# Layer 0's attention and its experts, two stages one after the other or one stage of turns

## The reference, cut to what matters

```python
x = x + _L0_gnn_ref(_layernorm(x), adj, W, a)            # graph attention, softmax over 64 nodes
x = x + _L0_ffn_ref(_layernorm(x), Wg, bg, W1, b1, W2, b2)
x = x + _L1_gnn_ref(_layernorm(x), adj, ...)             # three gated recurrent steps
x = x + _L1_ffn_ref(_layernorm(x), ...)                  # 16 experts of width 256, two for each token

def _L0_ffn_ref(x, Wg, bg, W1, b1, W2, b2):              # E = 8 experts, K = 2, hidden width 512
    topk_scores, topk_idx = jax.lax.top_k(x @ Wg.T + bg, K)
    combine = sum over K of softmax(topk_scores) * one_hot(topk_idx, E)
    for e in range(E):
        h = relu(x @ W1[e].T + b1[e])
        out = out + combine[..., e:e + 1] * (h @ W2[e].T + b2[e])
```

## Time and profile before

| | us |
|---|---|
| median of 3 runs | 1134.66 (1134.47 to 1137.16) |
| the profiled execution | 1134.32 |
| its span, first to last instruction | 1132.6 |
| PE busy | 977.3 (86%) |
| DVE busy | 766.8 (68%) |
| POOL busy | 601.0 (53%) |
| ACT busy | 578.4 (51%) |
| mean granted PE clock | 0.917 of 2.4 GHz |

### The profile page before, as it was taken

The page is one execution under the profiler, slowest core; times in us unless marked ns, Lnnn a source line. Parts: engine busy times, 40 slices in busy tenths (PEclk is TensorE's granted clock), DMA queues, the critical chain, the costliest instruction groups (busy, mean ns, idle before and its releaser), DMA issues. The chain is left out here.

```text
span 1132.6 us, 27053 instructions
## 1 busy us (share of the span) xinstructions
PE 977.3 (86%) x6816; PEld 802.3 (71%) x6817; DVE 766.8 (68%) x2985; ACT 578.4 (51%) x1469; POOL 601.0 (53%) x622
## 2 busy tenths in 40 slices
PE   4677776699999999859999999999985899999980
PEld 3666665499999999825555555555553789999980
DVE  3666666476666666437788888888975555555548
ACT  3777776333434343225555665565553334444455
POOL 2277777475555555510135554545545677767670
PEclk8777877699999999959999999999996899999995
DMA  9511111242222222130230321303010634333349
GB/s 229 201 49 47 49 47 54 71 115 78 70 67 72 69 69 69 41 124 0 75 89 24 96 69 54 101 29 121 25 42 31 130 107 112 93 91 90 90 143 365
DMA packets 109669, 99.08 MB, mean 87 GB/s; under 512 B 33424, under 2 KB 94480, under 8 KB 109328
## 3 DMA queue, kind: packets, MB, share of 16 engines
q1 hardware_dynamic: 92432, 62.83, 20.7%
q0 software_dynamic: 17152, 35.29, 9.3%
HBM read 55.44 MB, written 42.62 MB: 87 GB/s over the span
## 5 line engine op out<-in xcount | busy, mean ns | idle before, releaser
L1680 POOL DMA_INDIRECT result<-e_y,e_ids x280 | 280.2, 1001 | 164.2 <-issue 80.6
L415 POOL DMA_INDIRECT queue<-rows,slots x256 | 263.7, 1030 | 173.1 <-issue 121.2
L1711 PE MATMUL e_ps_h<-e_xT,e_up_of 128*128 128x128 f32 x2240 | 277.2, 278 | 3.0 <-DVE e_hT L1824 2.8
L1711 PEld LDWEIGHTS e_ps_h<-e_xT,e_up_of 128*128 128x128 f32 x2240 | 264.9, 194 | 4.0 <-issue 3.0
L1726 PE MATMUL e_ps_y<-w_sb,e_hT 128*128 x1664 | 208.3, 275 | 0.0
L1726 PEld LDWEIGHTS e_ps_y<-w_sb,e_hT 128*128 128x128 f32 x1664 | 196.8, 192 | 0.2 <-issue 0.2
L1750 ACT ACTIVATE e_hT<-e_ps_h,b_sb 128x128 f32<-128x128 f32 x272 | 77.9, 368 | 112.7 <-PE e_ps_h L1711 112.7
L1781 DVE COPY e_up_of<-w_sb 128x512 f32 x280 | 112.4, 441 | 4.1 <-issue 0.4
L1809 DVE TENSOR_SCALAR e_hT<-e_ps_h,b_sb 128x128 f32<-128x128 f32 x272 | 76.4, 343 | 32.8 <-PE e_ps_h L1711 32.6
L1824 DVE TENSOR_TENSOR e_hT<-e_ps_h,e_gate 128x512 f32<-128x512 f32 x72 | 49.7, 690 | 71.1 <-ACT e_gate L1759 71.0
L1759 ACT ACTIVATE e_gate<-e_ps_h 128x512 f32<-128x512 f32 x72 | 43.0, 597 | 96.8 <-PE e_ps_h L1711 95.5
(11 more groups left out here) (217 smaller groups left out, 1783.5 us busy)
## 6 DMA issues: line engine op xcount, KB each, us to landing
xq<-queue SPq DMA_DIRECT2D x280, 64.5 KB
g_y<-result SPq DMA_DIRECT2D x20, 512.0 KB, 4.0
result<-e_y,e_ids POOLq DMA_INDIRECT x280, 2.3
x_res<-x SPq DMA_DIRECT2D x16, 256.0 KB, 3.8
w_sb<-w SPq DMA_DIRECT2D x2, 2048.0 KB, 12.0
queue<-rows,slots POOLq DMA_INDIRECT x256, 2.5
w_sb<-w SPq DMA_DIRECT2D x16, 256.0 KB
rows<-result SPq DMA_DIRECT2D x8, 512.0 KB, 8.2
```

The costliest lines, as they stand in the source:

```text
L415: pool.indirect_dma_start(out=queue, out_offset=bass.IndirectOffsetOnAxis(ap=c.slots[q][:, k, t:t + 1], axis=0), in_=c.rows[q][:, k, t, :] ...
L1680: pool.indirect_dma_start(out=result, out_offset=bass.IndirectOffsetOnAxis(ap=ids[at_down.k][:, t, :].bitcast(U32), axis=0), in_=y[at_down ...
L1711: last = pe.matmul(ps_h[b][:, t, q * P:(q + 1) * P], up_of[at_up.k % 4][:, t, q * P:(q + 1) * P], xT[at_up.k % 4][:, t, :], start=True, st ...
```

## The change

The two stages become one, `gat_and_experts`, written out as 23 turns without a loop. In turn T, PE projects and mixes group T, turns group T-1's normalised rows, and scores and ranks T-2; four places in the turn hold an expert slot each. Slot p is in turn T, place j, with p = 4T + j - 22. In a slot's step PE turns the rows of slot p, forms the up products of p-1 and the down products of p-2 (lags of 1 and 2 in place of 2 and 4, with two buffers in place of four).

The first 56 slots are blocks of 256 rows of one expert, so that one load (1 DMA in place of 2), one copy of weights and up products with 256 columns serve both tiles; the last 12 are pairs of tiles of 128 as before, out of what is left at the end. The table is made in 14 batches of four blocks, from the counts after groups 2, 3, up to 15 (`TokenTables`, on one partition; batch b in turn b+4); the engines that need the experts' numbers load a word of each batch into a register (`TileExperts`), and SP reads the rows straight out of the table. Before the first load of a batch SP waits until the rows of group b+2 have landed.

In POOL's queue row sends and result sends take turns: two of a group, two of a slot. Attention has fewer PSUM buffers: one, `ps_t`, for all three kinds of transposes, and the projection, the scores and the ranks lie in the mix's two banks, with waits between them. Pads, the counting of landed tiles and the first loads of the next stage stay as they were, in their new places. Semaphores of the results' second half are new (`sent_first`).

```diff
+DOUBLE = 2 * P
+FOUR = 4
+DOUBLES = 56
+SINGLES = 24
+FIRST_SLOT = 22
...
-            gat_and_routing(nc, c, x, adj, gat_w, gat_wT, gat_a2, gate0_w, gate0_b, weights, small_weights, tables[0])
-            experts(nc, c, 0, c.queue0, c.result0, E0, H0 // P, up, down, up_b, down_b, tables[0], (NG - 2, NG - 1), adj, None)
+            gat_and_experts(nc, c, x, adj, gat_w, gat_wT, gat_a2, gate0_w, gate0_b, weights, small_weights, up_b, down_b)
...
+    def __call__(self, slot, t):
+        tables, tile = self.tables, slot.p if slot.double else (slot.p - DOUBLES) * PAIR + t
+        key = (slot.double, tile // FOUR)
+        if key not in self.words:
+            if slot.double:
+                self.eng.wait_ge(tables.made, tile // FOUR + 1)
+            else:
+                self.eng.wait_ge(tables.singles_made, 1)
+            source = tables.words if slot.double else tables.single_words
+            self.words[key] = self.nc.values_load_multi_w_load_instructions(
+                source[0:1, tile // FOUR:tile // FOUR + 1], engines=[self.eng.engine], min_val=0,
+                max_val=(1 << (BITS * FOUR)) - 1, skip_runtime_bounds_check_because="four experts of four bits each")[1][0]
+        return (self.words[key] >> (BITS * (tile % FOUR))) & (tables.n - 1)
...
-        ps_h = pb("ps_h", [P, GN])
-        ps_p = pb("ps_p", [P, GN])
-        ps_r = pb("ps_r", [P, GN])
-        ps_q = pb("ps_q", [P, 512])
-        scores_ps = ps_q[:, 0:G * E0]
-        ranks_ps = ps_q[:, G * E0:G * E0 + (G + 1) * E0]
+        ps_x, ps_y = (pb(name, [P, 512])[:, 0:DOUBLE] for name in ("ps_x", "ps_y"))
+        ps_up = [pb(f"ps_up{b}", [P, 512]) for b in range(2)]
+        ps_h = ps_o[:, 0, :]
+        scores_ps = ps_o[:, 0, 0:G * E0]
+        ranks_ps = ps_o[:, 1, 0:(G + 1) * E0]
...
+        def stages(T, j):
+            p = FOUR * T + j - FIRST_SLOT
+            return slot_of(p), slot_of(p - 1), slot_of(p - 2)
...
-            begin_experts(nc, sp, c, table, c.queue0, 0, E0, NG - 4)
+            for p in range(pairs):
+                slot = Slot(p)
+                if slot.double and p % FOUR == 0:
+                    batch = p // FOUR
+                    sp.wait_ge(tables.made, batch + 1)
+                    for s in range(0 if batch == 0 else batch + 2, batch + 3):
+                        wait_landed(sp, c, s % TURN, s // TURN + 1)
+                    starts = values(tables.rows, p, FOUR, E0 * REGION - DOUBLE)
+                if p == DOUBLES:
+                    sp.wait_ge(tables.padded, 16 * (E0 + 1))
+                    sp.wait_ge(tables.singles_made, 1)
+                if not slot.double and (p - DOUBLES) % FOUR == 0:
+                    starts = values(tables.single_rows, (p - DOUBLES) * PAIR, FOUR * PAIR, E0 * (REGION + P) - P)
+                if p >= HELD:
+                    sp.wait_ge(ids_copied, p - HELD + 1)
+                    alone(sp, c)
+                if slot.double:
+                    sp.dma_start(xq[p % HELD][:], c.queue0[bass.ds(starts[p % FOUR], DOUBLE), :]
...
-                    queue_rows(pool, c, c.queue0, g4.b)
-            staged(pool, body)
+            for T in range(turns):
+                for j in range(FOUR):
+                    s = group(T - 2 if j else T - 3)
+                    if s is not None:
+                        send_rows(s, 2 * (j - 1) if j else 6)
+                    at_down = stages(T, j)[2]
+                    if at_down:
+                        send_results(at_down)
...
+            def begin(slot):
+                v.wait_ge(x_turned, slot.p + 1)
+                if slot.p >= UNROLL:
+                    for t in range(PAIR):
+                        v.wait_ge(sent[t][slot.k], before[t][slot.k] + 16 * (slot.p // UNROLL))
+                v.tensor_copy(ids[slot.k][:], xq[slot.p % HELD][:, :, D:ROW]).then_inc(ids_copied, 1)
+                if slot.p >= 2:
+                    v.wait_ge(h_made, 2 * (slot.p - 1))
+                for t in range(1 if slot.double else PAIR):
+                    last = v.tensor_copy(up_of[slot.b][:, t * wide:(t + 1) * wide],
+                                         up[:, bass.ds(expert_of(slot, t) * wide, wide)])
+                last.then_inc(up_copied, 1)
...
+            def relu(slot):
+                v.wait_ge(h_made, 2 * slot.p + 2)
+                if slot.p >= 2:
+                    v.wait_ge(y_made, slot.p - 1)
+                if slot.double:
+                    for q in range(2):
+                        last = v.tensor_scalar(hT[slot.b][:, (2 + q) * DOUBLE:(3 + q) * DOUBLE],
+                                               ps_up[1][:, q * DOUBLE:(q + 1) * DOUBLE],
+                                               up_b[:, bass.ds(expert_of(slot, 0) * chunks + 2 + q, 1)], 0.0, ALU.add,
+                                               ALU.max)
...
-            staged(v, body)
+            for T in range(turns):
+                g, before_g, two_back, next_g = group(T), group(T - 1), group(T - 2), group(T + 1)
+                batch = T - 4
+                now, at_up, at_down = stages(T, 0)
+                if two_back is not None:
+                    route(two_back)
+                if now:
+                    begin(now)
+                rest(at_up, at_down)
+                if before_g is not None:
+                    update(before_g)
+                if T == NG + 2:
+                    tables.singles_1(v, c)
+                now, at_up, at_down = stages(T, 1)
+                if g is not None:
+                    attend(g)
+                if now:
+                    begin(now)
+                if two_back is not None:
+                    place(two_back)
+                rest(at_up, at_down)
+                if before_g is not None:
+                    stats(norm2, VN2, before_g)
+                    aggregate(norm2, VN2, before_g)
+                if T == NG + 2:
+                    tables.singles_2(v, c)
+                now, at_up, at_down = stages(T, 2)
+                if before_g is not None:
+                    shift(norm2, VN2, AN2, before_g)
+                if now:
+                    begin(now)
+                if next_g is not None:
+                    stats_1(next_g)
+                    aggregate(norm1, VN1, next_g)
+                rest(at_up, at_down)
+                if next_g is not None:
+                    mask(next_g)
+                if T == NG + 2:
+                    tables.singles_3(v, c)
+                if 0 <= batch < tables.batches:
+                    wait(v, VK, "carried", batch + 2)
+                    tables.doubles_1(v, c)
+                now, at_up, at_down = stages(T, 3)
+                if next_g is not None:
+                    shift(norm1, VN1, AN1, next_g)
+                if g is not None:
+                    mixed(g)
+                if now:
+                    begin(now)
+                if 0 <= batch < tables.batches:
+                    tables.doubles_2(v, c)
+                rest(at_up, at_down)
+                if 0 <= batch < tables.batches:
+                    tables.doubles_3(v, c, batch)
+                if T == NG + 2:
...
-            staged(act, body)
+            for T in range(turns):
+                g, before_g, next_g = group(T), group(T - 1), group(T + 1)
+                now, at_up, _ = stages(T, 0)
+                if g is not None:
+                    copy_turned("x", g, xnT)
+                if now:
+                    turn_out(now)
+                if at_up:
+                    relu(at_up)
+                now, at_up, _ = stages(T, 1)
+                if g is not None:
+                    copy_e(g)
+                if now:
+                    turn_out(now)
+                if g is not None:
+                    copy_h(g)
+                if at_up:
+                    relu(at_up)
+                if g is not None:
+                    exps(g)
+                if before_g is not None:
+                    inverse_std(norm2, VN2, AN2, before_g)
+                now, at_up, _ = stages(T, 2)
+                if g is not None:
+                    copy_turned("p", g, pT)
+                if now:
+                    turn_out(now)
+                if before_g is not None:
+                    normalise_2(before_g)
+                if at_up:
+                    relu(at_up)
+                if next_g is not None:
+                    inverse_std(norm1, VN1, AN1, next_g)
+                now, at_up, _ = stages(T, 3)
+                if before_g is not None:
+                    copy_turned("r", before_g, rT)
+                if now:
+                    turn_out(now)
+                if next_g is not None:
+                    normalise_1(next_g)
+                if at_up:
+                    relu(at_up)
+                if before_g is not None:
+                    copy_rows(before_g)
+                if g is not None:
+                    elus(g)
+                if T == NG + 1:
+                    act.wait_ge(product_made, 1)
```

(86 more changed lines are left out.)

690 lines of the change are left out of this document (428 added, 262 removed).

## The result

| us | before | after |
|---|---|---|
| median (lowest to highest, 4 runs each) | 1135.65 (1134.47 to 1137.16) | 1100.97 (1099.68 to 1102.61) |
| the profiled execution, its span | 1134.32, 1132.6 | 1102.61, 1100.9 |
| attention and layer 0's experts, start to PE's last down product | 10.6 to 476.8 | 10.75 to 448.0 |
| the next stage's first DVE row | 485.99 | 456.95 |
| mean granted PE clock | 0.917 | 0.929 |

The ratio is 0.9695, 95% interval 0.968 to 0.971: 34.7 us faster, where I forecast 14.3.

The account below looks back on a forecast made before the run. DVE was taken to bound the mixed turns: turn 6 begins at 110 us, ten turns of 23.3 reach 343, then 61 to 404 and 58 to 462.5, which is 14.3 earlier than 476.8. Forecast 1120 us, range 1097 to 1154.

Parts of the forecast that it names:

- DVE's turn: Turns 6 to 15: DVE's work and waits take 23.3 us a turn and are the bound; ten turns 233.
- The group's steps: DVE in a mixed turn: routing, place, statistics, scores, update, mask and shifts of the groups take 10.1 us.
- The four slots: DVE in a mixed turn: ids, copy, relus and bias add take 2.0 us per expert slot, 8.1 for four.
- The tables: DVE in a mixed turn: a batch's tables, 16 tiny operations in 11 dependent steps, take 3.0 us.
- The wait for ACT's logarithm and exponential: DVE in a mixed turn: the shift of group T-1 waits 0.7 us for ACT.
- Rival 1: Turns 6 to 15: PE and POOL bind, DVE's steps overlapping; a turn of 21.2 us, 1099 in all; chance 0.20.
- Turns 0 to 5: Attention chain, slots only in turn 5: 80 us for turns 0 to 4, 19 for turn 5; turn 6 begins at 110.
- Turns 16 to 18: After the last attention group: POOL's 30 remaining sends, landing, load and two slots take 61 us, to 404.
- Turns 19 to 22: The last expert slots: PE alone at 3.8 us a pair, 58 us, to 462.5.
- Rival 2: Mixed turns: a batch's first load comes late and PE stands; a turn of 26.5 us, 1152; chance 0.33.
- Rival 3: Mixed turns: no overlap, each turn pays its chain (17) and slots (14.8), 32 us; 1207; chance 0.05.
- The rule on the shared port: DVE's two-port copies lock out POOL's sends; nothing added; by it POOL's turn would be 22.6 us, still under 23.3.

Follow-up runs that it names:

- e8: Four 512-column fills more on DVE per turn 6 to 15, one behind each slot's bias add, against the kernel after: 1112.69 us, ratio 0.979.
- e9: e4 with slots 2 to 41 leaving out the last quarter of the down product on PE: 1090.62 us, ratio 0.960.
- e5: The kernel after without overlap, first slot in turn 18 when all groups are routed (FIRST_SLOT 72): 1213.44 us, ratio 1.069.
- e7: e4 with slots starting one place earlier (FIRST_SLOT 21): 1088.42 us; two places earlier (20): 1170.63 us.
- e4: The kernel after, with POOL sending all eight rows of a group together in place 1, results behind them: 1089.02 us, ratio 0.960.

## Why the prediction was wrong

**The failed term is DVE's turn.** It was taken at 23.3 and as the bound; turns 6 to 15 took 212.4 in place of 233, 20.6 less, and PE set them. PE's end came 14.5 ahead of the forecast: the other stretches took some 6 more than forecast. Term by term, in the turn from 193.54 to 214.37 on DVE, by the distance from the first row's start to the start of what follows:

- The group's steps: 9.1 for 10.1 (route 1.8, place 0.8, statistics 2.6, scores 1.3, update 1.4, reciprocal and product 0.8, mask and shifts 0.4).
- The four slots: 6.8 for 8.1. Here the sum of durations misled most: 0.43 + 0.87 + 0.41 = 1.71 of the earlier trace rows's kind of rows take 1.45 from 197.93 to 199.38, since most start 0.07 to 0.09 before the last one's end.
- The tables, with the 0.27 behind them: 3.0 for 3.0. The register load: 0.45 for 0.9.
- The wait for ACT's logarithm and exponential: 0.6 for 0.7.

These make 19.9 where the same terms were forecast at 22.8; e8's 22.5 less 2.8 is 19.7, and e9's 20.2 less its 0.3 of waits is 19.9. The 0.5 for handoffs was no work of DVE's; in this turn the waits on ACT's scores and on PE are 0.9, and they are not what holds the turn. I had the overlap in hand, in that the group's busy time of before was 7.8, and put the whole difference to 10.1 down to steps that stand behind each other.

**Rival 1 is what happened**, at its number: a turn of 21.2, 1099. The number was in part luck. Rival 1 let POOL (21.0, from a quotient that is 1.32 and not 1.31) set the turn with PE (20.4) under it. Measured, PE needs 20.9 (a group 6.0 where I took 5.6) and sets it; POOL needs 20.7. DVE is under PE by 1.0, not under POOL by 0.5. "Three engines at 96% and more, in order" was the ground against it; in after PE's losses by that are 0.4 a turn.

**Turns 0 to 5**: 108.6 for 110, right in the sum. Turn 1 (13.8 for 16) and turn 5 (17.8 for 19) were shorter, turns 2 to 4 longer (17.3 to 17.8 for 17; groups at 38.24, 56.01, 73.51, 90.81). e5 shows 17.1 without slots.

**Turns 16 to 18**: 67 for 61. The chain was the right one: place(14) ended 8 us into turn 16, and 41.2 went by from the first row send of group 14 to the end of group 15's last (39.3 forecast); from there to PE's transposes it took 4.5 (6.2 forecast). Three things were left out. POOL began those rows 3.1 after place(14), as group 13's last rows and results still stood in its queue. Among the 30 sends POOL then waited for results that were not made yet, with rows ready behind them, for 2.3, 1.2 and 0.8 us (the 0.3 of issue included):

```profile
341.67 1.00 POOL L1001 DMA_INDIRECT result<-a_y,a_ids  x1 [2.32 <-DVE a_y L1157]
```

And PE's waits cost more than they last: three of 2.9 to 3.7, where I had one, each with slots at a lower clock behind it. From slot 52 to turn 19 it took 10.5 where I had 7.5.

**Turns 19 to 22**: 59.7 for 58, a block's slot 3.73 and a pair's 3.79 where I had 3.8; the pipeline's end was a little longer. **The next stage** began 9.0 behind PE's end (9.2 forecast): right.

**Rival 2** did not happen, and e7 shows how near it was. **Rival 3** (1207) did not happen either; e5, where nothing overlaps, gives 1213.

**The rule on the shared port.** I added nothing for it, since the sends' means were equal in the two stages of before, 1014 and 1009 ns. Both means hold its cost. A send that is left alone takes 0.96. In before, 30 of the 95 sends from 260 to 440 us take 1.07 to 1.20, and each of the 30 began while DVE copied 512 columns; here the second of two copies, until 266.61:

```profile
265.85 0.76 DVE L1781 COPY e_up_of<-w_sb 128x512 f32 x2
266.30 1.14 POOL L1680 DMA_INDIRECT result<-e_y,e_ids  x1 [1.26 <-DVE e_y L1816]
```

In after 16 of 135 sends from 140 to 320 us take 1.03 to 1.46. Each began under one of four kinds of DVE rows, all with their operands in SBUF: the update, the copy of 512 columns, the mask, and the first step on the scores:

```profile
200.10 0.69 DVE L1084 SCALAR_TENSOR_TENSOR x_res<-a_elu,a_xz 128x512 f32<-128x512 f32 x1
200.17 1.46 POOL L430 DMA_INDIRECT queue<-rows,slots  x1 [0.30 <-issue]
```

The send is longer by what is left of that row at its start, less 0.13 (0.62 here, and 0.50 longer). Of 20 sends that began under a relu, which reads PSUM, and of 11 under the statistics or the row maxima, none is longer. All this makes 4.2 us in 135 sends, 0.5 a turn: POOL's 20.7 is 16 sends at 1.264 and this. So the lock that the Trainium skill describes (SBUF — State Buffer, Who interferes with whom) is there, but at 0.5 us a turn and not 1.6, since only a send that begins under such a row waits. It did not decide the turn here, as PE needs 0.2 more. What the Trainium skill says of regimes with different bounds (Perfetto Trace Analysis, Optimization Strategy) agrees with e5 against after, 1213 and 1101.

## What to carry to other kernels

Cost an in-order engine by the distance between starts in a dense stretch, not by a sum of durations: here DVE's turn came out 17% too high (23.3 for 19.9) and named the wrong bound. Where several engines are nearly full, one addition that is larger than the slack proves nothing; add less than the slack, add it elsewhere, and take work away. Then look who waits for whom before a time that equals another engine's work is called its bound: in e9 POOL was full and nobody waited for it yet. Two equal means don't show that an effect is absent; compare the rows that meet it with those that don't. Where a queue carries both what the next stage waits for and what nobody waits for (POOL's rows and results), put the first kind ahead.

## What the runs showed of the hardware that was not expected

- PE's pauses cost twice in these turns. Behind waits of 3.66, 2.92 and 3.10 the next 6.7 to 7.4 us ran at a granted clock of 0.58, 0.77 and 0.55, and the eight up products took 3.62 and 3.26 for 1.89. Not every pause does it: e4's of 3.16 at 364.41 lies in a stretch with a mean clock of 1.00.
- A fill and a drain on POOL between sends cost 2.1 to 2.5 us, of which the fill was 0.54; on DVE the same pair cost 0.70, of which 0.485 was the fill.
- An indirect send that begins under DVE's update, copy of 512 columns, mask or first step on the scores is longer by the rest of that row less 0.13 us: in after by up to 0.50 on 0.96. Where such a row begins later than the send (34 sends of after from 140 to 320 us) the send keeps its 0.96.
